# Cross-attention and experts on one core: q and k sent through a scratch in memory instead of being spread by TensorE, weights fetched on another queue

## The reference, cut to what matters

```
q = einsum('bsd,ed->bse', layernorm(x), Wq) -> 16 heads of 8
k, v = the same of ctx (16 x 64 x 128) with Wk, Wv
attn = softmax(q k^T / sqrt(8), axis=heads)
x = x + (attn v) Wo^T
h = layernorm(x); shared: 2 experts for all; routed: 2 of 8 experts by score
x = x + h + shared(h) + weighted routed(h)        # each expert: 128 -> 512 -> gelu -> 128
```

## Time and profile before

| | us |
|---|---|
| median of 3 runs (527.93 to 542.43) | 528.89 |
| the profiled execution | 525.64 |
| its span | 523.8 |
| PE, DVE, ACT, POOL busy | 356.3, 327.1, 279.5, 286.9 |

### The profile page before, as it was taken

One profiled execution on the slowest core, in us unless ns is written; L12 is line 12 of the kernel. 1 busy time (PEld: TensorE's weight loads), 2 busy tenths in 40 slices (PEclk: granted clock), 3 DMA queues, 4 the chain that ended last, 5 costly groups with the idle time before them and its releaser, 6 DMA issues.

```text
span 523.8 us, 11740 instructions
## 1 busy us (share of the span) xinstructions
PE 356.3 (68%) x3844; PEld 255.5 (49%) x3845; DVE 327.1 (62%) x639; ACT 279.5 (53%) x523; POOL 286.9 (55%) x293
## 2 busy tenths in 40 slices
PE   5786477768675766469602589969788888888700
PEld 2342244445453643156302357658677777777600
DVE  7994579999999596128104685455554554565437
ACT  3977533477776533158302358845654564465336
POOL 7598765687878427710771700515555655655610
PEclk9999659898988679569855889999999999999955
DMA  8900000000000001100110111032222222221057
GB/s 307 324 13 5 2 11 12 11 11 11 12 1 0 1 11 48 50 16 2 50 53 18 42 51 43 26 87 62 60 67 68 65 63 56 71 66 55 23 201 281
DMA packets 34250, 30.89 MB, mean 59 GB/s; under 512 B 13460, under 2 KB 30487, under 8 KB 33824
## 3 DMA queue, kind: packets, MB, share of 16 engines
q1 hardware_dynamic: 29664, 21.89, 14.0%
q0 software_dynamic: 4544, 8.44, 4.8%
HBM read 17.55 MB, written 12.62 MB: 58 GB/s over the span
## 4 chain that ended last, share of the span: by engine, by line
PE 39%; DVE 22%; issue 11%; ACT 10%; another core or an unknown queue 8%; POOL 5%; DMA 3%; ACTq 1%; SPq 0%; DVEq 0%; POOLq 0%
PE banks L1455 5%; DVE Mx L853 4%; ACT E L716 3%; PE banks L1468 3%; PE banks L1467 3%; POOL E L400 2%; PE banks L1255 2%; PE banks L1384 2%; DVE E L1143 2%; PE banks L1388 2%; PE banks L1386 2%; PE banks L1469 2%; ACT kRep L714 2%; PE banks L1453 2%
## 5 line engine op out<-in xcount | busy, mean ns | idle before, releaser
L479 POOL DMA_INDIRECT results<-E,qRep x78 | 83.4, 1069 | 75.3 <-DVE E L1135 52.5
L469 POOL DMA_INDIRECT gathered<-xs,slot x64 | 64.7, 1010 | 99.3 <-DVE xs L1021 54.3
L714 ACT ACTIVATE kRep<-banks 128x512 f32<-128x512 f32 x78 | 47.8, 613 | 68.3 <-PE banks L1455 66.6
L676 ACT ACTIVATE kRep<-banks 128x512 f32<-128x512 f32 x64 | 38.6, 603 | 82.3 <-PE banks L1370 37.9
L400 POOL TENSOR_TENSOR E<-E,rZ 128x1024 f32<-128x1024 f32 x32 | 68.3, 2157 | 24.6 <-DVE rZ L861 24.6
L1384 PE MATMUL banks<-wprojL,E 128*128 128x128 f16 x256 | 51.1, 231 | 40.2 <-DVE E L926 35.6
L1143 DVE TENSOR_TENSOR E<-kRep,E 128x512 f16<-128x512 f32 x78 | 53.9, 691 | 24.4 <-ACT E L716 16.6
L1467 PE MATMUL banks<-wprojL,E 128*128 x312 | 59.5, 219 | 11.4 <-DVE E L1143 9.5
L926 DVE TENSOR_TENSOR E<-kRep,E 128x512 f16<-128x512 f32 x64 | 43.6, 691 | 37.6 <-ACT E L677 32.4
L1468 PE MATMUL banks<-wprojH,E 128*128 x312 | 58.2, 218 | 3.0 <-issue 2.6
L1469 PE MATMUL banks<-wprojH,E 128*128 x312 | 58.2, 218 | 2.2 <-issue 2.2
(11 more groups left out here) (203 smaller groups left out, 932.1 us busy)
## 6 DMA issues: line engine op xcount, KB each, us to landing
qRep<-gathered SPq DMA_DIRECT2D x39, 129.0 KB, 1.9
qRep<-results SPq DMA_DIRECT2D x8, 512.0 KB, 6.7
E<-in_wfc_t SPq DMA_DIRECT2D x1, 2560.0 KB, 13.6
X<-in_x SPq DMA_DIRECT2D x4, 512.0 KB, 6.5
kPad<-kRep SPq DMA_DIRECT2D x128, 8.0 KB
out<-X SPq DMA_DIRECT2D x8, 256.0 KB, 3.8
xs<-in_wproj_t SPq DMA_DIRECT2D x1, 1280.0 KB, 14.2
results<-E,qRep POOLq DMA_INDIRECT x78
```

Source lines behind the costliest of these rows:

```text
L469: g.indirect_dma_start(out=gathered, out_offset=bass.IndirectOffsetOnAxis(ap=slot[:, k, i:i + 1], axis=0), in_=xs[:, i, :], in_offset=None ...
L479: g.indirect_dma_start(out=results, out_offset=bass.IndirectOffsetOnAxis(ap=xg[:, k, h, 2 * D:ROW].bitcast(I32), axis=0), in_=yg[:, k, h, ...
```

## The change

- The `select` matrices, the spreads on TensorE and the copies out of them on ACT and DVE are gone, and so is `kRep`. Each step's q parts (`qs`) are stored to a scratch in memory (`q_rows`: 4 DMAs of 128 rows of 1 KB for each step n) and loaded from there into `qRep` (4 DMAs of 64 rows of 4 KB, 256 KB each). k goes to `k_rows` with one DMA, and `kPad` is filled from there with 8 DMAs of 16 rows for each pair instead of 16 of 8 rows; the source is read twice over for each. To get the order of rows, `wk` and `wq` are first copied on DVE with their columns in another order (`rows_first`).
- `high_q` of step n now waits until the stores of step n - 1 have landed (`q_stored`), since `qs` is used again.
- The weights are issued from POOL's queue in 8 DMAs, between its constants, after the second quarter of x has landed. Their split is divided: for 8 of the 20 blocks POOL scales and makes the low part and ACT the high part; for the other 12 ACT scales while it makes the high part, and DVE makes the low part in one instruction (`lows`). Only the first 6 high parts and 2 low parts come before the first unit; the rest stand in units 0 to 3.
- The last two of the four q steps (`project_q`, `high_q`, `low_q`, one of the transposes) move into units 0 and 1.
- The first norm of a step's first pair is made on DVE instead of ACT for all steps; the table for exp is loaded on ACT before the first unit; ACT waits before the exp of unit 3 for all stores of q, whose tile shares memory with that exp's output.

The diff, cut ("..." marks what is left out):

```diff
-PAD_PARTS = 4 * QUARTER
+PAD_PARTS = 2 * QUARTER
 SKIP = 1 << 20
 NBANK = 8
 BANK = 512
@@ -87,8 +87,8 @@
         negI = sb("negI", [P, P], BF16)
...
         qRep = sb("qRep", [P, PAIRS, HH, S], F16)
@@ -147,35 +147,37 @@
...
         NR = 12
...
 
 
...
-        proj_f32 = [E_flat[:, 7424:7424 + F].rearrange("p (e n) -> p e n", e=1),
-                    xs_flat[:, 2816:2816 + 5 * 2 * F].bitcast(F32).rearrange("p (e n) -> p e n", e=5),
-                    x2_flat[:, 0:4 * 2 * F].bitcast(F32).rearrange("p (e n) -> p e n", e=4)]
+        raw_w = [E_flat[:, 3072:6144].rearrange("p (e n) -> p e n", n=F),
+                 hid[:],
+                 xs_flat[:, 10 * D:10 * D + 6 * 2 * F].bitcast(F32).rearrange("p (e n) -> p e n", n=F),
...
         iota8 = sb("iota8", [P, EXPERTS])
 
 
@@ -184,7 +186,6 @@
         v_ps = [banks[:, i, :] for i in (2, 3)]
         t_ps = [banks[:, i, :] for i in (4, 5)]
...
-            sp.dma_start(wfc_f32, wfc_t).then_inc(wfc_loaded, 16)
...
-            for part, (lo, hi) in zip(proj_f32, PROJ_PARTS):
-                sp.dma_start(part, wproj_t[:, lo:hi]).then_inc(wproj_loaded, 16)
-            sp.wait_ge(masks, BASICS)
-            for b in range(2):
-                for half in range(2):
...
+            def output_weights(halves):
+                for b, half in halves:
...
-            ov = out.rearrange("(a b p c) d -> p a b (c d)", a=PAIRS, p=P, c=2)
-            Xo = X[:].rearrange("p a b c d -> p a b (c d)")
-
-            def pad_k(pair):
+
+            def pad_k(pair, quarters=(0, 1, 2, 3)):
 
                 j = pair % 2
                 if pair > 1:
...
-                for b in range(2):
-                    for odd in range(2):
-                        for i in range(QUARTER):
-                            r = slice(64 * b + 16 * i + DK * odd, 64 * b + 16 * i + DK * odd + DK)
-                            sp.dma_start(kPad[r, j, odd, :, b], kRep[r, pair]).then_inc(kPad_loaded[j], 16)
...
+                for quarter in quarters:
+                    b, odd = divmod(quarter, 2)
+                    for low in range(2):
+                        r = 64 * low + 32 * b + 16 * odd
+                        src = k_rows[low, quarter].rearrange("d g (a s) -> d g a s", s=SK)[:, :, pair]
+                        sp.dma_start(kPad[r:r + 16, j, odd, :, b], src.unsqueeze(0).broadcast_to([2, DK, HH, SK])
+                                     ).then_inc(kPad_loaded[j], 16)
+
+            def store_q(n):
+                for low, done in enumerate((qhi_ready, qlo_ready)):
+                    for j in range(2):
+                        sp.wait_ge(done, 2 * n + j + 1)
+                        sp.dma_start(q_rows[2 * n + j, :, low].rearrange("b d g n -> b (d g) n"), qs[:, j, low]
+                                     ).then_inc(q_stored[j], 16)
+
+            def load_q(n):
+
+                for j in range(2):
+                    pair = 2 * n + j
+                    sp.wait_ge(q_stored[j], 32 * n + 32)
+                    src = q_rows[pair].rearrange("b l d g n -> (b l d) (g n)")
+                    for i in range(2):
+                        sp.dma_start(qRep[64 * i:64 * i + 64, pair].rearrange("p g q -> p (g q)"), src
+                                     ).then_inc(q_loaded[pair], 16)
+
+            sp.wait_ge(masks, BASICS)
+            output_weights(((0, 0), (0, 1)))
+            sp.wait_ge(klo_ready, 2)
+            sp.dma_start(k_rows.rearrange("l q d (g h) n -> (q d g) l h n", h=2), ks).then_inc(k_stored, 16)
+            output_weights(((1, 0), (1, 1)))
             sp.wait_ge(masks, BASICS + 2)
-            for side in range(2):
-                sp.wait_ge(spread_out[side], 2)
-            for pair in range(PAIRS):
+            sp.wait_ge(k_stored, 16)
+            pad_k(0, (0, 1))
+            store_q(0)
+            pad_k(0, (2, 3))
+            load_q(0)
+            store_q(1)
+            pad_k(1)
+            load_q(1)
+            store_q(2)
+            pad_k(2)
+            load_q(2)
+            store_q(3)
+            pad_k(3)
+            load_q(3)
+            for pair in range(4, PAIRS):
                 pad_k(pair)
...
+            for i, (raw, (lo, hi)) in enumerate(zip(raw_w, WEIGHT_PARTS)):
+                if i == 0:
+                    pool.wait_ge(x_loaded[1], 16)
+                for odd in range(2):
+                    w = (wfc_t, wproj_t)[i // 2][:, lo + odd:hi:2]
+                    pool.dma_start(raw[:, odd::2], w).then_inc(weights_loaded[i], 16)
...
+            def scaled(part):
+                pool.wait_ge(weights_loaded[part], 32)
+                for e in range(4):
+                    w = raw_w[part][:, e]
+                    g.tensor_tensor(w, w, consts[:, 2, 0:1].broadcast_to([P, F]), ALU.mult).then_inc(weight_scaled, 1)
+
+            def low_parts(part, scaled_before):
+                for e in range(4):
+                    pool.wait_ge(weight_scaled, scaled_before + e + 1)
+                    pool.wait_ge(high_ready[part], e + 1)
+                    g.tensor_tensor(low_w[part][:, e], raw_w[part][:, e], high_w[part][:, e], ALU.subtract
+                                    ).then_inc(low_ready[part], 1)
+
+            scaled(1)
+            scaled(3)
+            low_parts(1, 0)
+            low_parts(3, 4)
...
+            def highs(part, lo, hi):
+                act.wait_ge(weights_loaded[part], 32)
+                if part % 2:
+                    act.wait_ge(weight_scaled, 8 if part == 3 else 4)
                 for e in range(lo, hi):
-                    act.wait_ge(wfc_scaled, e + 1)
-                    s.activation(wfcH[:, e], wfc_f32[:, e], ACT.Copy).then_inc(wfcH_ready, 1)
...
+                    s.activation(high_w[part][:, e], raw_w[part][:, e], ACT.Copy, scale=1.0 if part % 2 else W_SCALE
+                                 ).then_inc(high_ready[part], 1)
...
-                        act.wait_ge(spread[0], 2 * n + j + 1)
-                        act.wait_ge(spread[1], 2 * n + j + 1)
+                        act.wait_ge(q_stored[j], 32 * n)
...
-            def spread_k_out(half):
-                act.wait_ge(spread[0], half + 1)
-                s.activation(kRep[:, :, half * QUARTER:half * QUARTER + 2].rearrange("p a g s -> p g a s"),
-                             spread_ps[0].rearrange("p g (a s) -> p g a s", s=SK), ACT.Copy).then_inc(spread_out[0], 1)
-
             deviation(0)
             first_norm(0, False)
-            spread_k_out(0)
+            for i in range(2):
+                act.wait_ge(v_ready, i + 1)
+                s.activation(V[:, 4 * i:4 * i + 4], v_ps[i], ACT.Copy).then_inc(V_ready, 1)
             copy_xnT(0)
             deviation(1)
-            spread_k_out(1)
             first_norm(1, True)
             high_q(0, False)
-            high_w(0, 2)
             deviation(2)
+            copy_xnT(1)
+            first_norm(2, True)
+            high_q(1, True)
+            deviation(3)
+            s.activation(tables[:, 1:2], eps[:], ACT.Exp)
+            highs(0, 0, 2)
+            copy_xnT(2)
+            first_norm(3, True)
+            highs(0, 2, 6)
...
+                    if first and k == 1:
+                        act.wait_ge(low_ready[0], 2)
+                    if first and k == 2:
+                        act.wait_ge(low_ready[0], 6)
+                    if first and k == 3:
+                        act.wait_ge(k_stored, 16)
+                        for j in range(2):
+                            act.wait_ge(q_stored[j], 32 * (PAIRS // 2))
                     exps(u, k, not first)
+                    if first and k == 0:
+                        high_q(2, True)
+                        copy_xnT(3)
+                        highs(1, 0, 4)
+                        spread_v(0, 0)
+                    if first and k == 1:
+                        high_q(3, True)
+                        highs(3, 0, 4)
+                        spread_v(1, 1)
+                    if first and k == 2:
+                        highs(2, 0, 6)
...
+            for part, (lo, hi) in enumerate(WEIGHT_PARTS):
+                act.wait_ge(low_ready[part], hi - lo)
...
-            v.memset(select, 0.0).then_inc(select_ready, 1)
-            dve.wait_ge(select_ready, 1)
-            dve.wait_ge(masks, BASICS)
...
+            def rows_first(out, w):
+
+                return v.tensor_copy(out.rearrange("p (h x g) -> p h x g", h=2, g=QUARTER),
+                                     w.rearrange("p (h g x) -> p h x g", h=2, g=QUARTER))
...
+            def lows(part, lo, hi):
+                for e in range(lo, hi):
+                    dve.wait_ge(high_ready[part], e + 1)
+                    v.scalar_tensor_tensor(low_w[part][:, e], raw_w[part][:, e], W_SCALE, high_w[part][:, e],
+                                           ALU.mult, ALU.subtract).then_inc(low_ready[part], 1)
...
-            def spread_q_out(n, sides=(0, 1)):
-                for j in range(2):
-                    for side in sides:
```

(88 more changed lines are left out.)

167 lines of the change are left out of this document (30 added, 137 removed).

## The result

| | before | after |
|---|---|---|
| median of runs | 529.66 us | 538.47 us (536.07 to 540.16, 4 runs) |
| ratio, 95% interval | | 1.0192 [1.0151, 1.0233] |
| profiled execution, and its span | 525.64, 523.8 | 536.07, 534.3 |
| Max 0, Max 4 | 54.45, 82.88 | 44.90, 92.96 |

The ratios leave out the runs in the chip's slower state, such as 542.43 us among the four of the kernel before (527.93 to 542.43). Run again beside other kernels, the changed kernel stood at 1.0204 [1.0163, 1.0246]. The forecast was 517.5, with 538 as the upper end. *Max n* is the start of the maximum of unit n on DVE, and an *interval* is the distance from one Max to the next. The difference of spans is 10.5 us; at Max 4 it is 10.1, at Max 5 and at the last unit 11.0, and the expert stage takes back 0.5.

The account below looks back on a forecast made before the run. Preparation was taken as crowded, not stalled, and filled units as bound by DVE. 18.0 won less 6.2 lost is 11.8, less 0.5 is 11.3: 514.3 on the profiled execution, 517.5 for runs; range 507 to 538.

Parts of the forecast that it names:

- first exp earlier: Preparation up to unit 0's exp: it starts at 41.2 instead of 59.23, 18.0 us earlier.
- exp 0 to Max 1: Unit 0: maximum 1 starts 3.8 us after the exp's start, against 3.17 before, a loss of 0.6.
- Max 1 to Max 2: Unit 1: DVE's list with `low_q(3)` takes 10.4 us against 6.60 before, a loss of 3.8.
- Max 2 to Max 3: Unit 2: three `lows` fit within the 8.03 us of before, a loss of 0.
- Max 3 to Max 4: Unit 3: DVE has no gap in its 5.85 us, so three `lows` cost 1.8.
- Stores of q: Preparation: step 0's four store DMAs leave SP from about 20 and land at 32, between 23.4 and 34.3.
- if SP's list, not landings, holds the loads: Sign that the prediction is wrong, for the loads of q on SP; no size given.
- Lows: DVE's low parts of weights in units 2 and 3: about 0.6 us each, priced from a 0.63 us subtraction from PSUM.
- Rival B: DMAs of q and pads: few engines carry them, ACT waits for stores; time 527 or 545; chance 0.38 (0.18 lower, 0.20 upper).
- POOL's issues: Preparation: eight direct DMAs take 10 us, moving the masks from 12.3 to 23; cost 0, at most 1.
- ACT's list: Preparation, from the landing of q's stores to the first exp: 8.7 us of ACT work, exp ready at 40.7.
- the clock: Units 0 to 3 may all run at 1.2 GHz; counted as 0, at most 2 us.

Follow-up runs that it names:

- Experiment 5: Changed kernel with q's stores of steps 2 and 3 moved ahead in SP's order, still on four engines: 536.21 us, ratio 1.0073 to the kernel before.
- experiment 3: Changed kernel with q's scratch laid out low/high part outermost, so stores have 128 rows on both sides and pads 8 rows: 534.81 us, ratio 1.014 to the kernel before.
- Experiment 4: Changed kernel with q's stores issued from POOL's queue instead of SP's: 530.31 us, ratio 1.0033 to the kernel before.
- Experiment 8: Changed kernel with DVE's low parts made from one input (results not the reference's): 540.12 us in a single run; made by a reduction, ratio 1.011 to the kernel before.
- experiment 1: Changed kernel with six high parts and six `lows` moved from units 2 and 3 into unit 1: 530.3 us, ratio 1.0037 to the kernel before.
- experiment 2: Changed kernel with POOL issuing the weights' loads only after k's store has landed: 541.85 us, ratio 1.0237 to the kernel before.

## Why the prediction was wrong

The account is at Max 4, where it closes. Forecast: 18.0 won, 6.2 lost, so 11.8 ahead. Measured 10.1 behind. The 21.9 between them lie in four terms.

| term | forecast | measured | off by |
|---|---|---|---|
| first exp earlier (its start) | 18.0 (41.2) | 11.3 (47.97) | 6.8 |
| exp 0 to Max 1 | 3.8 | 3.83 | 0 |
| Max 1 to Max 2 | 10.4 | 18.51 | 8.1 |
| Max 2 to Max 3 | 8.03 | 11.34 | 3.3 |
| Max 3 to Max 4 | 7.65 | 11.31 | 3.7 |

**Stores of q (14.9 of it, the failed step).** "The nearest row is `wo`: I take 32", and ACT's last wait for step 0's stores ended at 37.79. I had three quantities in one number: when they leave, how they are carried, when they are there. The stores could not leave at 20, as SP was held by k's landing (9.90) and by pads whose issues took 1.77 each, not 0.69: they left at 29.09. That price of issue is a term that I took from pads of another form. Then four engines carried them, and they landed 8.7 after that, where I had allowed 12: by luck the two errors cancel in part, and 9.1 us late in leaving became 5.8 late in landing. My own sign, "if SP's list, not landings, holds the loads", was there too: `load_q(0)` went out at 38.27, behind the last pad (38.22) and not at the landing. The larger slip is in unit 1. I priced the same landing there only through `low_q(3)` on DVE and took ACT's `high_q(3)` as free to run: it overwrites what `store_q(2)` reads, just as `high_q(1)` waits for step 0's. The prediction walked this wait once, for step 1, and not again for step 3, behind 8 pads and 4 loads on SP. Experiment 5 gives the order's share, 6.3 us at Max 4, experiment 3 that of the engines, 6.0; both overlap in the wait. Experiment 4 starts the first exp at 44.14, so 3.8 of its 6.8 hang on SP's list and queue.

**Lows (7.0).** "For `lows` no row has the operation; 0.63 is the subtraction from PSUM of the same size": alone that was nearly right (0.686). But its nearest row reads one input from PSUM, and the place where I put it, units 2 and 3, is where POOL normalises. Measured 1.72 and 1.89 each. Experiment 8 shows the cause: with a form that POOL does not hold up, the two intervals are 6.6 us shorter. The cover that I gave unit 2 wasn't there in full either: without any `lows` its interval is 8.50 in experiment 1, and with unhindered ones 8.64.

**Rival B** was right in its rule (four engines, two) and partly in its mechanism (ACT waits for stores over 5 us), wrong in its price and place. While pads run alone they are issued every 0.65 us (8 in 5.22 at 99.83) and keep two engines full; by rival B's own measure a packet is then busy 14.1% x 16 x 2 us / 350 = 12.9 ns, under its lower bound of 14. Its 27 ns, and the time of 545 with them, were twice what the packets took. The last stores (issued at 72.02 to 74.4, landed by about 81 as the windows show) held nobody, and the exp of unit 3 waited for TensorE until 85.20. The wait was two units earlier, for step 2. That its two prices, 527 and 545, stand on either side of the result bears nothing out.

**What held.** POOL's issues (6.2 us for eight, forecast 10) and masks (19.78, forecast 23) cost nothing. ACT's list between the store's landing and the first exp was as counted: 37.79 to 47.97, of which 2.27 is a wait for TensorE: 7.9 of work against 8.7. The intervals from unit 5 on held, and an expert stage that changed by 0.5 us. I counted the clock as 0. It was 0.54 and 0.50 in 60 to 70 and 70 to 80 us, as it was 0.50 before in 60 to 70; what it costs here no run separates.

## What to carry to other kernels

When a value goes through memory, price four things apart: when its producer is done, what stands ahead of its issue in that queue, how many engines the two shapes allow, and who must wait to reuse the buffer; then walk every later step of the same loop and not only the first. Put VectorE's two-input work (and fast single-source work) where GpSimd computes nothing, or make it a form that needs one port. A change that mends one stage fully can still lose what it moves elsewhere: here 9.6 us won ahead of unit 0 were all real.

## What the runs showed of the hardware

- The issue of a DMA on SP isn't of fixed length. A pad of 16 rows took 0.65 us with idle engines, up to 3.0 with four stores' packets under way (32 to 38 us), and 3.1 in the mean beside the weights' loads (experiment 2). Pads of 8 rows took 0.65 in the median and 0.86 at most beside the same loads (experiment 3). Why the form matters so much to the issue no run shows.
- A VectorE instruction that needs the shared port waits for the whole of GpSimd's: 686 ns become 2320 in the median, and POOL's own instructions rise from 2.13 in the median to 2.33 in the mean. A reduction of the same size (676 ns) is not held up.
- Storing 128 KB with rows outermost on both sides ran at 267 GB/s, with four blocks outermost on one side at 95 (four of them at a time).
